# Start of a four-layer hybrid kernel: the qkv load on ScalarE's queue, a warm-up of 19 matmuls on a cleared tile, the first fold ahead of the turned x, and two changes of order

## The reference, cut to what matters

```python
def _L0_attn_a_ref(x, qkv, o_proj, gamma, beta):
    mu = jnp.mean(x, axis=-1, keepdims=True)
    var = jnp.mean((x - mu) ** 2, axis=-1, keepdims=True)
    x_norm = (x - mu) / jnp.sqrt(var + EPS) * gamma + beta
    q = x_norm @ qkv[:, :KEY]
    k = x_norm @ qkv[:, KEY:2 * KEY]
    v = x_norm @ qkv[:, 2 * KEY:]
    scores = jnp.einsum('bsk,btk->bst', q, k) * scale
    scores = jnp.where(causal[None], scores, -jnp.inf)
    attn = jax.nn.softmax(scores, axis=-1)
    out = (attn @ v) @ o_proj
    return out + residual

x = x + _L0_attn_a_ref(_layernorm(x, axis=-1), qkv, o_proj, gamma, beta)
x = x + _L0_ffn_ref(_layernorm(x, axis=-1), gate_w, up_w, down_w, gate_scale, up_scale, down_scale)
x = x + _L0_attn_b_ref(_layernorm(x, axis=-1), D_param, log_dt, A_real_log, A_imag, C_re, C_im)
x = x + _L0_ffn_ref(_layernorm(x, axis=-1), gate_w, up_w, down_w, gate_scale, up_scale, down_scale)
```

## Time and profile before

| | us |
|---|---|
| median of 3 runs | 122.87 |
| lowest and highest of the runs | 122.67 and 123.37 |
| the profiled execution, its own time | 123.42 |
| its span in the profile | 121.6 |
| PE busy | 115.3 |
| DVE, POOL, ACT busy | 98.2, 83.8, 77.4 |

### The profile page before, as it was taken

The page is one execution under the profiler, slowest core; times in us unless marked ns, Lnnn a source line. Parts: engine busy times, 40 slices in busy tenths (PEclk is TensorE's granted clock), DMA queues, the critical chain, the costliest instruction groups (busy, mean ns, idle before and its releaser), DMA issues.

```text
span 121.6 us, 2132 instructions
## 1 busy us (share of the span) xinstructions
PE 115.3 (95%) x685; PEld 79.9 (66%) x685; DVE 98.2 (81%) x231; ACT 77.4 (64%) x147; POOL 83.8 (69%) x163
## 2 busy tenths in 40 slices
PE   5999999999999998999999999999999999999960
PEld 5798889467678666644678545577445589756650
DVE  0458999996998996969797898999899985797482
ACT  0452599968465368858938269785489665589700
POOL 2205599999999878997943588689976782037731
PEclk9999999999999999999999999999999999999996
DMA  3989920000000000000000000000000000000505
GB/s 98 363 244 411 356 59 0 0 0 0 0 0 3 0 8 0 0 0 0 0 0 5 0 0 0 0 3 5 0 0 0 3 0 5 0 0 0 172 0 172
DMA packets 5614, 5.80 MB, mean 48 GB/s; under 512 B 1618, under 2 KB 4836, under 8 KB 5604
## 3 DMA queue, kind: packets, MB, share of 16 engines
q1 hardware_dynamic: 4632, 5.53, 13.2%
q10 hardware_dynamic: 972, 0.15, 0.7%
HBM read 4.63 MB, written 1.05 MB: 47 GB/s over the span
## 4 chain that ended last, share of the span: by engine, by line
PE 69%; DVE 12%; ACT 5%; POOL 5%; DMA 4%; issue 3%; SPq 0%; POOLq 0%; DVEq 0%
PE psum L1326 18%; PE psum L1360 11%; PE psum L1265 8%; PE psum L1240 7%; PE psum L1202 6%; DMA qkv_sb<-in_qkv 4%; PE psum L1195 3%; PE psum L1340 3%; PE psum L1188 3%; PE psum L1158 3%; DVE stats L749 2%; ACT h_rows L583 2%; PE psum L1287 2%; DVE x_plus L1018 2%; PE psum L1151 2%
## 5 line engine op out<-in xcount | busy, mean ns | idle before, releaser
L637 ACT ACTIVATE gated<-psum,scales 128x512 f32<-128x512 f32 x24 | 16.3, 680 | 12.2 <-PE psum L1326 9.9
L1360 PE MATMUL psum<-down,f_head 128*128 128x256 bf16 x96 | 22.0, 273 | 0.0
L1360 PE MATMUL psum<-down,f_tail 128*128 128x256 bf16 x96 | 22.0, 273 | 0.0
L1049 DVE SCALAR_TENSOR_TENSOR fused<-psum,up_scales_fit,gated 128x512 f32<-128x512 f32 (+1 forms) x25 | 17.8, 716 | 3.2 <-PE psum L1326 1.9
L447 POOL TENSOR_TENSOR f_tail<-fused,f_head 128x512 f16<-128x512 f32 x10 | 11.8, 1182 | 10.5 <-ACT f_head L643 9.2
L643 ACT ACTIVATE f_head<-fused 128x512 f16<-128x512 f32 (+1 forms) x25 | 15.2, 608 | 2.6 <-DVE fused L1049 2.3
L295 POOL TENSOR_TENSOR rstd<-var_eps,neg_half 128x2 f32<-128x2 f32 (+1 forms) x15 | 11.7, 777 | 2.2
L1057 DVE TENSOR_TENSOR f_tail<-fused,f_head 128x512 f16<-128x512 f32 (+1 forms) x15 | 10.1, 676 | 3.8 <-ACT f_head L643 3.7
L1326 PE MATMUL psum<-h_head,up 128*128 128x512 f16 x44 | 13.1, 379 | 0.0
L1326 PE MATMUL psum<-h_head,gate 128*128 128x512 f16 x44 | 13.1, 379 | 0.0
L1326 PE MATMUL psum<-h_tail,gate 128*128 128x512 f16 x44 | 13.1, 379 | 0.0
(11 more groups left out here) (183 smaller groups left out, 271.7 us busy)
## 6 DMA issues: line engine op xcount, KB each, us to landing
x_in<-in_x SPq DMA_DIRECT2D x4, 256.0 KB, 5.8
qkv_sb<-in_qkv SPq DMA_DIRECT2D x1, 768.0 KB, 4.4
gate_raw<-in_gate_w SPq DMA_DIRECT2D x1, 768.0 KB, 7.7
up_raw<-in_up_w SPq DMA_DIRECT2D x1, 768.0 KB, 9.2
down_raw<-in_down_w SPq DMA_DIRECT2D x1, 768.0 KB, 10.9
out<-x_in SPq DMA_DIRECT2D x3, 256.0 KB, 2.1
wo_sb<-in_o_proj SPq DMA_DIRECT2D x1, 256.0 KB, 5.5
down_scale_all<-in_down_scale SPq DMA_DIRECT2D x1, 128.0 KB, 6.0
```

The source lines that it names most:

```text
L637: act.activation(gated[:, m % 2, :], psum[:, BANK_GATE[m % 2], :], ACT.Silu, scale=gate_scales[:, m:m + 1]).then_inc(gated_ready, 1)
L1049: dve.scalar_tensor_tensor(out=fused[:, m % FUSED, cols], in0=psum[:, BANK_UP[m % 2], cols], scalar=up_scales_fit[:, m:m + 1], in1=gated[: ...
L1360: last = pe.matmul(down_columns(n, t), part[:, m, t * P:t * P + P], down16[:, m, :], start=(m == 0 and (t % 2 == 0 or n == 2 * B - 1) and ...
```

## The change

Six edits, all in the first 50 us of the program:

1. ACT's queue issues qkv, then x tiles 2 and 3, then o_proj, as its first instructions. SP issues x tiles 0 and 1, and behind it the six small loads that ACT had, then the rest as before.
2. The warm-up is 19 `matmul` instructions on a new tile `warm`, which DVE clears as its first instruction; before it was 17 `transpose` instructions on `ident`.
3. ACT copies all three transposed parts of qkv; DVE copies none.
4. PE runs `fold` for `wqk` ahead of `turn_z_half(0)`; ACT copies `wqk` ahead of `xn_half(0)`.
5. DVE runs `g_second_half` and `xn_second` ahead of `row_max(0)` and `row_max(1)`.
6. POOL runs `inverse_std(1, 2, 2)` ahead of `taps_begin`.

```diff
-WARM_UP = 17
+WARM_UP = 19
@@ tiles, semaphores
+        warm = sb("warm", [P, P])
+        warm_ready = sem("warm_ready")
-        w_turned_pe, q_v_turned, k_turned = sem("w_turned_pe"), sem("q_v_turned"), sem("k_turned")
+        w_turned_pe, w_turned_ready = sem("w_turned_pe"), sem("w_turned_ready")
@@ SP
             load_x(0)
-            load_chunks(qkv_sb[:], qkv, qkv_loaded)
-            load_x(1)
-            load_chunks(wo_sb[:], o_proj, wo_loaded)
+            load_rows(param_rows, (gamma, beta, d_param), params_loaded)
+            sp.dma_start(e_in[:, 0:HN].rearrange("p (c n) -> p c n", c=C),
+                         a_real_log.rearrange("(c p) n -> p c n", p=P)).then_inc(a_loaded, 16)
...
             load_x(2)
             load_x(3)
@@ POOL
             inverse_std(1, 0, 2, negative_mean=True)
+            inverse_std(1, 2, 2, negative_mean=True)
             taps_begin()
-            inverse_std(1, 2, 2, negative_mean=True)
@@ ACT
-            load_row(0, gamma)
-            load_row(1, beta)
-            load_row(2, d_param)
...
+            act.dma_start(qkv_sb[:], qkv.rearrange("(c p) n -> p c n", p=P)).then_inc(qkv_loaded, 16)
+            act.dma_start(x_in[:, 2:4, :], x_tiles[:, 2:4, :]).then_inc(x_loaded[1], 16)
+            act.dma_start(wo_sb[:], o_proj.rearrange("(c p) n -> p c n", p=P)).then_inc(wo_loaded, 16)
             turned(0)
+            turned(1)
             turned(2)
-            xn_half(0)
             act.wait_ge(wqk_made, 1)
             act.activation(wqk[:].rearrange("p c n -> p (c n)"), psum[:, BANK_WQK, :], ACT.Copy).then_inc(wqk_ready, 1)
+            xn_half(0)
@@ DVE
+            dve.memset(warm[:], 0.0).then_inc(warm_ready, 1)
             first_stats(0)
             normalise((0, 1))
-            copy_k()
             copy_params()
...
             grid_end(0)
+            g_second_half()
+            xn_second()
             row_max(0)
             row_max(1)
-            g_second_half()
-            xn_second()
@@ PE
-            pe.wait_ge(ident_ready, 1)
             def warm_up(times):
 
                 for n in range(times):
-                    pe.transpose(column(BANK_NORMS, 0, P), ident[:], ident[:])
+                    pe.matmul(column(BANK_NORMS, 0, P), warm[:], warm[:], start=True, stop=True)
 
+            pe.wait_ge(warm_ready, 1)
             warm_up(WARM_UP)
+            pe.wait_ge(ident_ready, 1)
...
             pe.transpose(column(BANK_PARAMS, 0, 3 * C), param_rows[:], ident[0:3 * C, 0:3 * C]).then_inc(params_turned, 1)
+            pe.wait_ge(w_turned_ready, 2)
+            fold(BANK_WQK, 0, lambda kc: w_turned[:, 1, kc, :]).then_inc(wqk_made, 1)
             turn_z_half(0)
-            pe.wait_ge(q_v_turned, 1)
-            pe.wait_ge(k_turned, 1)
-            fold(BANK_WQK, 0, lambda kc: w_turned[:, 1, kc, :]).then_inc(wqk_made, 1)
-            pe.wait_ge(q_v_turned, 2)
+            pe.wait_ge(w_turned_ready, 3)
             pe.wait_ge(wo_loaded, 16)
             fold(BANK_WVO, 2, lambda kc: wo_sb[:, kc, :]).then_inc(wvo_made, 1)
```

More of the change, by code:

```diff
@@ L242, in _ @@
             load_x(0)
-            load_chunks(qkv_sb[:], qkv, qkv_loaded)
-            load_x(1)
-            load_chunks(wo_sb[:], o_proj, wo_loaded)
+            load_rows(param_rows, (gamma, beta, d_param), params_loaded)
+            sp.dma_start(e_in[:, 0:HN].rearrange("p (c n) -> p c n", c=C),
+                         a_real_log.rearrange("(c p) n -> p c n", p=P)).then_inc(a_loaded, 16)
+            with nc.allow_non_contiguous_dma(reason="256 time steps, one per partition"):
+                sp.dma_start(e_in[:, HN:HN + C], log_dt.rearrange("(c p) -> p c", p=P)).then_inc(a_loaded, 16)
+            sp.dma_start(s4d_in[:, 1, :].rearrange("p (c n) -> p c n", c=C),
+                         a_imag.rearrange("(c p) n -> p c n", p=P)).then_inc(omega_loaded, 16)
             load_x(2)
@@ L495, in _ @@
         def _(act):
-            def load_row(n, vector):
-                act.dma_start(param_rows[C * n:C * n + C, :],
-                              vector.rearrange("(m p) -> m p", p=P)).then_inc(params_loaded, 16)
             def turned(w):
@@ L502, in turned @@
                 act.activation(w_turned[:, w, :, :].rearrange("p c n -> p (c n)"), psum[:, BANK_WT[w], :],
-                               ACT.Copy).then_inc(q_v_turned, 1)
+                               ACT.Copy).then_inc(w_turned_ready, 1)
             def xn_half(half):
@@ L762, in first_stats @@
                 tile_stats(0, [k, k + 1], x_in)
[L765 to L768, removed]
             def copy_params():
```

## The result

The changed kernel takes 126.88 us in the median of 4 runs (125.99 to 127.24), the kernel before 122.81 in 4 runs. The ratio is 1.030, 95% interval 1.0265 to 1.0338: 4.1 us slower by the medians, 3.7 by the ratio. The direction and both mechanisms were forecast, the size was not: 125.6 was given, and the median lies 0.1 us above the upper end of the range. The profiled execution, the slowest of the four, took 127.24 us with a span of 125.4, against 123.42 and 121.6. The ratios of this document leave out executions more than 1.5% above the fastest of the same kernel, which matters most for the POOL order alone, where four of twelve were.

The account below looks back on a forecast made before the run. PE was taken to bound the kernel, busy 115.3 of 121.6 us. T0 - 5.15 with T0 = 7.4 added 2.25 us to 123.42, giving 125.7; the predicted time was 125.6, range 124.2 to 126.8.

Parts of the forecast that it names:

- The warm-up's length: PE's start: 19 matmuls are 38 passes from about 1.0 us, 0.217 us each at the lower clock, 0.111 at the upper.
- T0: Moment the warm-up ends and PE's transposes of qkv start: taken as 7.4 us, against 5.64 before.
- R: Moment during PE's warm-up when TensorE's clock rises to its upper level: taken as about 5.5 us.
- rival 1: Clock rise during the warm-up unchanged or later, 7.0 to 8.0 us: 126.4 to 126.9 us; chance 0.17.
- rival 3: Real matmuls in the warm-up raise the clock sooner, at 3.0 to 4.5 us: 124.5 to 125.2 us; chance 0.19.
- The load of qkv: Initial loads: qkv lands 0 to 0.5 us earlier, hidden by the warm-up; gain taken as nothing.
- The fold first: First fold: PE idles 0.35 us ahead of it; DVE gets turned x later, PE waits 0.8 us before second make_g_half.
- The POOL order and bound: Near 47.5 us: about 0.5 us of the h_rows stop goes, but bound, with POOL 0.7 behind PE, delays h_tail.
- net 0 to 0.1: First gate_up: the wait for h_tail takes back the 0.5 us regained at h_rows, leaving 0 to 0.1 us.
- The DVE order: DVE's xn_second ahead of the row maxima: old order just in time; row maxima 1.3 us later, cost taken as zero.
- That nothing takes the delay back: Behind 68 us PE waits for work starting from its own results, so the delay stays whole.
- Rivals 4, 5 and 6: 4: one-pass instructions, 123.2-124.0 us, 0.06; 5: idle stretches absorb delay, 123-123.5, 0.06; 6: upper clock almost immediately, 122.0-122.3, 0.05.

Follow-up runs that it names:

- the POOL order alone: The kernel before with GpSimd's inverse_std(1, 2, 2) ahead of taps_begin, nothing else: ratio 0.9976 (0.9952 to 1.0000).
- ninth and tenth runs: VectorE's statistics of tiles 2 to 5 ahead of xn_half(0): in the changed kernel with ten warm-up matmuls, 123.51 us; in the kernel before with fold first, 123.56 us.
- third experiment: The kernel before with the first fold ahead of turn_z_half(0) and the copy of wqk ahead of xn_half(0): 125.72 us, ratio 1.0195.
- second experiment: The kernel before with the warm-up edit alone, 19 matmuls on the tile VectorE clears: 125.21 us, ratio 1.0153.

## Why the prediction was right or wrong

**The warm-up's length: right.** 38 passes, from 1.04 us, at 0.213 and 0.112 us (0.217 and 0.111 were used), over after qkv had landed. For a rise at 7.0 the working gave T0 = 8.15, and 8.20 was measured.

**The moment of the rise: mis-sized.** I took R about 5.5 and with it T0 = 7.4; the profile has R = 7.0. That is 0.8 us of the 1.3 that the forecast is short, and it is rival 1 that fits this profile (126.4). The other three executions, 125.99 to 127.19 us, do not show their rise. Taking PE's earlier start off the old R had no support: over thirteen of the fourteen profiles the passes change pace between 5.0 and 7.2 us, with no order by how early PE began (1.04 us: 5.5, 5.7, 6.5, 6.7, 6.8, 7.0, 7.1, 7.2; 1.5 us: 5.0, 5.1, 5.1, 6.2, 7.0). In the fourteenth, the POOL order alone, PE stood idle for 2.7 us until qkv landed, and the change came at 11.0. With real matmuls in the warm-up it came no sooner, and with transposes alone it came as well, so rival 3 fell. With 38 passes in front, this moment is worth half a microsecond for each microsecond (rises at 6.7, 7.0 and 7.2 us gave T0 = 8.09, 8.20 and 8.30); with a warm-up that ends early it moves only the 12 transposes.

**The load of qkv: wrong in sign, without effect.** "0 to 0.5 us earlier" was forecast; in this profile it landed at 5.9 against 5.6 (over all profiles the medians differ by 0.1 us). The first x landed 1.2 us later (statistics at 4.73 against 3.49), which was foreseen. Both were hidden as said. The saturated DMA engines were in the rows; that qkv might then land no earlier, or later, was not drawn from them.

**The fold first: right in its path.** DVE's xn_cols was forecast at T0 + 4.2 = 12.4 and started at 12.52; the second make_g_half at T0 + 12.1 = 20.3 and started at 20.34; make_g at T0 + 16.8 = 25.0 and started at 25.02. The view gives 0.55 us for the wait there, counted from the end of the matmul ahead; from start to start PE lost 0.71 (0.77 against 0.06), where I wrote 0.8. The ninth and tenth runs show the cause, VectorE's queue.

**The POOL order and bound: the second mis-sized term.** With T0 = 8.2 the sum puts h_tail's end at 51.1 + 3.05 = 54.15; PE got it at 54.7. `bound` started 4.35 us later, not 3.7. I had POOL only 0.7 us behind PE and let the new order add nothing. GpSimd's rows, now and then in the kernel before:

```profile
45.66 0.20 POOL L306 TENSOR_TENSOR neg_mean_rstd<-mean_rstd,rstd 128x2 f32<-128x2 f32 x1
45.97 0.19 POOL L296 TENSOR_SCALAR var_eps<-mean_var 128x2 f32<-128x2 f32 x1
...
47.43 0.19 POOL L306 TENSOR_TENSOR neg_mean_rstd<-mean_rstd,rstd 128x2 f32<-128x2 f32 x1
47.90 0.39 POOL L324 TENSOR_TENSOR s4d<-s4d 128x16 f32<-128x16 f32 x2 [0.27 <-issue]
...
48.83 1.10 POOL L324 TENSOR_TENSOR s4d<-s4d 128x16 f32<-128x16 f32 x2
```

```profile
41.84 0.20 POOL L300 TENSOR_TENSOR neg_mean_rstd<-mean_rstd,rstd 128x2 f32<-128x2 f32 x1
42.00 0.40 POOL L318 TENSOR_TENSOR s4d<-s4d 128x16 f32<-128x16 f32 x2
...
42.94 0.52 POOL L318 TENSOR_TENSOR s4d<-s4d 128x16 f32<-128x16 f32 x2
...
45.44 1.23 POOL L295 TENSOR_TENSOR rstd<-var_eps,neg_half 128x2 f32<-128x2 f32 x1
```

From the first of these rows to `bound` it is 5.65 us now and was 5.12. `inverse_std(1, 2, 2)`, moved forward, waits for the statistics of tile 3 (GpSimd's row at 45.97 follows DVE's, which runs from 45.70 to 45.88); before, the taps' work had covered that wait. And the taps start 0.47 us behind the row ahead of them, in place of 0.16, for which the view names no cause. The pair of 1.10 us, 0.58 longer than before, is no loss by itself: it runs beside VectorE's `down_raw` of 0.96 us, which before fell on the power of 1.23 us (0.71 elsewhere). All seven profiles with the new order have these 5.65 us, wherever the fold and however long the warm-up. With the old order it is 5.11 to 5.14 with the fold order of before and 5.45 with the fold first. So "net 0 to 0.1" was 0.6.

The half microsecond to be regained at h_rows did not come either: PE waits for probs_cols there instead, as in the POOL order alone. With the fold first, make_g to the first matmul on h_tail takes 29.76 us in the old POOL order (third experiment) and 29.71 in the new. The new order trades the wait for h_rows for one for h_tail.

With the warm-up's 0.8 and this 0.6 the sum of 125.7 becomes 127.1, against 127.24 for the profiled execution.

**The DVE order: right**, no change by itself; in the old order the copy of x was to be "just in time" with the fold first, and the third experiment has it about 0.3 us late. **That nothing takes the delay back: right**, 3.15 us at make_g became 3.8 at the first matmul on h_tail and stayed. **Rivals 4, 5 and 6 fell**: the row is x38, the delay is whole at the end, and the upper clock did not come at once.

## What to carry to other kernels

Count the passes of a warm-up, not its instructions, and make it end before the data it bridges can land; a float32 matmul here is twice a float32 transpose, and what runs beyond the wait is paid for, less what the upper clock gives back (in the second experiment the transposes started 2.7 us later and the kernel lost 1.9). When an operation moves back on one engine, look at what stands in the queues of the engines that wait for its result: 0.3 us of idle time on PE became 2.4 us, because VectorE held the next statistics behind a wait, and putting them ahead of it gave it back but for 0.2 us or so, which the runs cannot tell from nothing. When a wait goes away, look at what stands next: the stop at h_rows went, and the copy of the probabilities took its place. A load issued earlier into DMA engines that are already full gained nothing here and made the load in front of it 1.1 us later.

## What the runs showed of the hardware that was not expected

The moment at which TensorE's pace doubles moved between 5.0 and 7.2 us in executions of nearly the same start, and followed neither PE's first instruction nor its kind; behind an idle stretch of PE from 5.4 to 8.1 us it came at 11.0. The column of the granted clock showed 1.00 all the while, so the spacing of the passes is the surer sign. A float32 matmul of 128x128 left two passes, a float32 transpose one. The float32 128x128 passes of a matmul at the upper clock started 0.112 us apart, transposes 0.109.
